# V rows kept at 32 columns a head in DRAM, padded by the stage that writes them

## The reference

```
k = (key @ Wk.T + bk);  v = (value @ Wv.T + bv)           # cross attention, key = value = context
scores = einsum('bqhd,bkhd->bhqk', q, k) * 16 ** -0.5
attn = softmax(scores);  out = einsum('bhqk,bkhd->bqhd', attn, v)
x = x + out @ Wo.T + bo
h = x' + causal_attention(rmsnorm(x', g1))                # x' = layernorm(x), rotary q and k, same head sizes
y = h + moe(rmsnorm(h, g2))                               # 8 experts, top 2
```

## Time and profile before

| | us |
|---|---|
| median of 3 runs | 3302.17 (3297.82 to 3305.19) |
| the profiled execution | 3297.82, its span 3296.2 |
| `project_inputs`, first and last instruction of its work | 22.5 to 284.7 |
| cross attention | 289.1 to 1656.7 |
| `project_self` | 1670.0 to 1898.6 |
| self attention | 1903.5 to 2292.8 |

### The profile page before, as it was taken

One profiled execution on the slowest core, in us unless ns is written; L12 is line 12 of the kernel. 1 busy time (PEld: TensorE's weight loads), 2 busy tenths in 40 slices (PEclk: granted clock), 3 DMA queues, 4 the chain that ended last, 5 costly groups with the idle time before them and its releaser, 6 DMA issues. The chain is left out here.

```text
span 3296.2 us, 55561 instructions
## 1 busy us (share of the span) xinstructions
PE 2698.5 (82%) x14654; PEld 1323.0 (40%) x14655; DVE 1763.2 (53%) x2832; ACT 1458.2 (44%) x2927; POOL 490.7 (15%) x650
## 2 busy tenths in 40 slices
PE   7996999999999999999949879887340299999980
PEld 5662232323232323233225434443340177777760
DVE  4565876767676767677436656664222022222223
ACT  2331576767676767677723336565010022222210
POOL 2444000000000000000014421110223300000006
PEclk9996899999999999999979979999665699999995
DMA  6777544444454444454035456653444211100116
GB/s 211 215 233 133 70 62 67 62 66 63 62 64 62 63 63 63 62 63 61 17 115 185 159 121 133 133 133 102 149 150 155 84 32 32 32 32 32 32 47 183
DMA packets 524784, 313.32 MB, mean 95 GB/s; under 512 B 312112, under 2 KB 486848, under 8 KB 524480
## 3 DMA queue, kind: packets, MB, share of 16 engines
q1 hardware_dynamic: 492752, 256.93, 38.6%
q0 software_dynamic: 11392, 37.76, 3.5%
q10 hardware_dynamic: 20464, 16.40, 1.6%
HBM read 188.91 MB, written 121.26 MB: 94 GB/s over the span
## 5 line engine op out<-in xcount | busy, mean ns | idle before, releaser
L719 DVE TENSOR_REDUCE att_cross_neg_max<-att_cross_ps_s 128x1 f32<-128x802 f32 x1024 | 965.6, 988 | 350.9 <-PE att_cross_ps_s L636 349.2
L794 ACT ACTIVATE att_cross_probs<-att_cross_ps_st 128x512 f32<-128x512 f32 (+1 forms) x1664 | 901.2, 599 | 394.7 <-PE att_cross_ps_st L655 382.2
L655 PE MATMUL att_cross_ps_st<-att_cross_q_pack,att_cross_k_pack 99*128 99x512 bf16 (+1 forms) x1664 | 575.0, 391 | 37.3 <-issue 28.4
L636 PE MATMUL att_cross_ps_s<-att_cross_k_pack,att_cross_q_pack 96*128 96x401 bf16 x2048 | 547.9, 350 | 70.1 <-DVE att_cross_neg_max L719 29.5
L670 PE MATMUL att_cross_ps_o<-att_cross_probs,att_cross_v_tiles 128*32 128x512 f32 (+1 forms) x3328 | 453.5, 618 | 1.0
L636 PEld LDWEIGHTS att_cross_ps_s<-att_cross_k_pack,att_cross_q_pack 96*128 96x128 bf16 x2048 | 176.8, 100 | 420.5 <-DVE att_cross_neg_max L719 204.9
L655 PEld LDWEIGHTS att_cross_ps_st<-att_cross_q_pack,att_cross_k_pack 99*128 99x128 bf16 (+1 forms) x1664 | 163.1, 100 | 415.5 <-ACT att_cross_probs L794 293.2
L719 DVE TENSOR_REDUCE att_self_neg_max<-att_self_ps_s 128x1 f32<-128x128 f32 (+3 forms) x512 | 236.2, 489 | 148.7 <-PE att_self_ps_s L639 145.7
L794 ACT ACTIVATE att_self_probs<-att_self_ps_st 128x256 f32<-128x256 f32 (+3 forms) x512 | 208.2, 441 | 142.4 <-PE att_self_ps_st L658 136.6
L1744 DVE COPY moe_hiddenT<-moe_ps_h 128x256 f32<-128x256 f32 x142 | 60.3, 425 | 296.9 <-PE moe_ps_h L1654 296.9
L636 PE MATMUL att_self_ps_s<-att_self_k_pack,att_self_q_pack 96*128 96x128 bf16 (+3 forms) x512 | 158.7, 312 | 56.4 <-DMA att_self_q_pack<-q_parts 25.1
(11 more groups left out here) (208 smaller groups left out, 2901.7 us busy)
## 6 DMA issues: line engine op xcount, KB each, us to landing
att_cross_k_pack<-k_parts SPq DMA_DIRECT2D x192, 200.1 KB, 7.5
k_parts<-in_part SPq DMA_DIRECT2D x72, 256.0 KB, 3.1
in_rows<-in_ctx_dram SPq DMA_DIRECT2D x24, 512.0 KB, 4.4
v_rows<-in_v_biased SPq DMA_DIRECT2D x24, 512.0 KB, 2.9
att_cross_q_pack<-q_parts SPq DMA_DIRECT2D x192, 64.0 KB, 7.7
att_cross_v_tiles<-v_rows SPq DMA_DIRECT2D x128, 96.0 KB
att_self_k_pack<-k_parts SPq DMA_DIRECT2D x192, 64.0 KB, 3.1
att_self_q_pack<-q_parts SPq DMA_DIRECT2D x192, 64.0 KB, 3.1
```

Of the source, the lines that this page charges most:

```text
L636: last = nc.tensor.matmul(ps_s[bank][:, n, 0:w], qp[v.buf][0:SROWS, j, q * P:(q + 1) * P], kp[v.buf][0:SROWS, j, s:s + w], start=True, sto ...
L655: mm = nc.tensor.matmul(ps_st[bank_of_step[s]][0:rows, q0:SEQ], kp[u.buf][0:MROWS, j, t * P:t * P + rows], qp[u.buf][0:MROWS, j, q0:SEQ], ...
L719: nc.vector.tensor_reduce(nmax[v.odd][:, col, half:half + 1], ps_s[bank][:, 0:len(spans), 0:spans[0][1]], AX.XY, ALU.max, negate=True).the ...
L794: nc.scalar.activation(pr[0:rows, (u.odd * STEPS + s) % RING, q0:SEQ], ps_st[bank_of_step[s]][0:rows, q0:SEQ], ACT.Exp).then_inc(exp_done, 1)
```

## The change

V is kept in DRAM as the attention reads it: 16 heads of 32 columns, ones and zeros included, so a row of `v_rows` grows from 1 KB to 2 KB. The stages that write V keep buffers of this shape, `v_pad`, set the ones and zeros in them once on DVE, and write each head's 16 numbers with a stride. The attention loads four heads (512 bytes a row) with one DMA for the full tiles and one for the rest, and no longer sets ones and zeros.

```diff
+        vpad = [p.sb(f"v_pad{i}", [P, QT, HEADS, VW]) for i in range(2)]       # project_inputs
-                            sp.dma_start(dst, vb[st.item % 2][0:st.size, 0, :])
+                            sp.dma_start(dst, vpad[st.item % 2][0:st.size, 0, :, :].rearrange("p h v -> p (h v)"))
...
             def _(dve):
+                for i in range(2):
+                    nc.vector.memset(vpad[i][:, :, :, HD:VW], 0.0).then_inc(pads, 1)
+                dve.wait_ge(pads, 2)
+                for i in range(2):
+                    nc.vector.memset(vpad[i][:, :, :, HD:HD + 1], 1.0).then_inc(pads, 1)
+                dve.wait_ge(pads, 4)
                 dve.sem_inc(xT_ready, 2)
...
-                        last = nc.vector.tensor_tensor(vb[st.item % 2][0:m, t, :], ps_v[0:m, t, :], ...
+                        last = nc.vector.tensor_tensor(vpad[st.item % 2][0:m, t, :, 0:HD],
+                                                       ps_v[0:m, t, :].rearrange("p (h d) -> p h d", d=HD), ...
...
-        VLOADS = 16 * GH * ((1 if kv >= P else 0) + (1 if kv % P else 0))      # attention
+        VLOADS = 16 * ((1 if kv >= P else 0) + (1 if kv % P else 0))
                 def load_v(v):
-                    for j in range(GH):
-                        src = v_rows[v.batch, :, v.columns.start + j * HD:v.columns.start + (j + 1) * HD]
-                        if kv >= P:
-                            sp.dma_start(va[v.vbuf][:, 0:kv // P, j, 0:HD], ...
+                    if kv >= P:
+                        sp.dma_start(va[v.vbuf][:, 0:kv // P, :],
+                                     v_rows[v.batch, 0:kv // P * P, v.columns].rearrange("(t p) v -> p t v", p=P))
+                    if kv % P:
+                        sp.dma_start(va[v.vbuf][0:kv % P, kv // P, :], v_rows[v.batch, kv // P * P:kv, v.columns])
...
-                for k in range(VBUFS):
-                    nc.gpsimd.memset(va[k][:, :, :, HD + 1:VW], 0.0).then_inc(ones_set, 1)
-                    nc.gpsimd.memset(va[k][:, :, :, HD:HD + 1], 1.0).then_inc(ones_set, 1)
...
                 def take_v(b):                                                  # project_self
-                    nc.scalar.copy(vs[:, :, :].rearrange("p (c t) d -> p c (t d)", c=KC), ps_t[:, :, :])
+                    for t in range(QT):
+                        last = nc.scalar.copy(vpad[:, t, :, 0:HD],
+                                              ps_t[:, t // 2, t % 2 * DIM:(t % 2 + 1) * DIM]
+                                              .rearrange("p (h d) -> p h d", d=HD))
...
-    v_rows = dram("v_rows", [batches, CTX, DIM])
+    v_rows = dram("v_rows", [batches, CTX, HEADS * VW])
-    v2_rows = dram("v2_rows", [batches, SEQ, DIM])
+    v2_rows = dram("v2_rows", [batches, SEQ, HEADS * VW])
```

More of the change, by code:

```diff
@@ L381, in take_v @@
                     for t, m in st.tiles():
-                        last = nc.vector.tensor_tensor(vb[st.item % 2][0:m, t, :], ps_v[0:m, t, :], keep["bv"][0:m, :],
-                                                       ALU.add)
+                        last = nc.vector.tensor_tensor(vpad[st.item % 2][0:m, t, :, 0:HD],
+                                                       ps_v[0:m, t, :].rearrange("p (h d) -> p h d", d=HD),
+                                                       keep["bv"][0:m, :].rearrange("p (h d) -> p h d", d=HD), ALU.add)
                     last.then_inc(v_ready, 1)
@@ L474, in attention @@
         qp = [p.sb(f"q_pack{i}", [P, GH, SEQ], BF16) for i in range(BUFS)]
-        va = [p.sb(f"v_tiles{i}", [P, NT, GH, VW]) for i in range(VBUFS)]
+        va = [p.sb(f"v_tiles{i}", [P, NT, GH * VW]) for i in range(VBUFS)]
         pr = p.sb("probs", [P, RING, SEQ])
@@ L521, in __init__ @@
                 self.rows = slice(g * GR, (g + 1) * GR)
-                self.columns = slice(g * GR, (g + 1) * GR)
+                self.columns = slice(g * GH * VW, (g + 1) * GH * VW)
                 self.odd = r % 2
@@ L670, in products @@
                         nc.tensor.matmul(ps_o[j * VW:(j + 1) * VW, q0:SEQ],
-                                         va[u.vbuf][0:rows, t, j, :],
+                                         va[u.vbuf][0:rows, t, j * VW:(j + 1) * VW],
                                          pr[0:rows, (u.odd * STEPS + t * GH + j) % RING, q0:SEQ],
@@ L933, in project_self @@
         v_sent = p.sem("v_sent")
+        pads = p.sem("pads")
         SENT = 16 * 3
@@ L1026, in _ @@
             def _(dve):
+                nc.vector.memset(vpad[:, :, :, HD:VW], 0.0)
+                dve.drain()
+                nc.vector.memset(vpad[:, :, :, HD:HD + 1], 1.0).then_inc(pads, 1)
                 for s in (on_ready, x1_ready, rope_read, *rest_ready):
@@ L1106, in take_v @@
                     act.wait_ge(v_sent, (b + 1) * 16)
-                    nc.scalar.copy(vs[:, :, :].rearrange("p (c t) d -> p c (t d)", c=KC), ps_t[:, :, :])\
-                      .then_inc(v_ready, 1)
+                    for t in range(QT):
+                        last = nc.scalar.copy(vpad[:, t, :, 0:HD],
+                                              ps_t[:, t // 2, t % 2 * DIM:(t % 2 + 1) * DIM]
+                                              .rearrange("p (h d) -> p h d", d=HD))
+                    last.then_inc(v_ready, 1)
                 def high(w, b):
```

28 lines of the change are left out of this document (14 added, 14 removed).

## The result

The changed kernel takes 3324.26 us (median of five, 3319.75 to 3327.92), against 3297.82 for the kernel before in the same session: a ratio of 1.0070, interval 1.0055 to 1.0086. It is slower by 26 us in the medians, by 23 by the ratio; I had forecast +5.5 us, 3307.7, in a range from 3298 to 3317.

What follows compares the result with a forecast made beforehand. The prediction took PE to set the pace in all four stages; 0 (cross) - 2 (self) + 5.5 (ring) + 2 (clock) = +5.5 us, giving 3303.3, or 3307.7 in the median's terms, range 3298 to 3317.

Steps and rivals of the forecast that it cites:

- V's loads in the self attention: Self attention: 4 DMAs a unit become 1, shortening PE's waits for the maxima rows; -2 us, bounds 0 and -6.5.
- V's loads in the cross attention: Cross attention: 8 DMAs a unit become 2, old and new price hidden under PE's work; 0 us.
- The ring: `project_self`: V's larger store delays the h0 store's landing and next residual, 1.37 us in four turns; +5.5, bounds 0 and +11.3.
- PE's clock in `project_self`: `project_self`: PE's pause before L994 grows to 2.8 us, so the granted clock falls once; +2 us.
- New memsets: Projections and `project_self`: new DVE memsets of 2.4 and 1.2 us stay hidden; 0 us.
- DVE's stride: Projections, bias add L382: strided writing of V costs 0, upper bound 12 us; as a rival 3318 us, chance 0.05.
- POOL's memsets: Memsets that leave POOL: PE comes to its first product long after them; 0 us.
- V's store in the projections: Projections: store 13.1 MB larger, DMA share from 0.74 to about 0.87 of 1.08; 0 us.
- ACT's four strided copies: `project_self`: ACT's copy of 1.01 us becomes four, at most 1.6 us, before a 4.33 us gap; 0 us.
- The slower one: Rival in `project_self`: larger store at 185 GB/s or two clock falls, +9 to +12.5, 3311 to 3315 us; chance 0.23.
- The faster one: Rival: self attention's maxima rows come in time in every unit (-6.5), V's store hidden; 3295.7 us, chance 0.10.
- The condition under which I had called the prediction wrong: Wrong if ring keeps 23.6 us, L382 grows, or PE's waits in either attention change by more than 6.5 us.

Runs made afterwards that it cites:

- v_store_last: Changed kernel with V's store in `project_self` issued behind those of x1 and h0: 3319.20 us against 3302.00 for the kernel before, ratio 1.0051.
- pads_on_pool: Changed kernel with the two padding memsets of `project_self` on POOL instead of DVE: 3311.59 us against 3292.86 for the kernel before, ratio 1.0060.
- half_load: Changed kernel with V's self-attention load cut to its first two tiles, the others set to ones: 3305.44 us against 3292.86 for the kernel before, ratio 1.0044.
- best_plain: Kernel before, unpadded; four k/q loads ahead of the maxima rows, eight behind, V's load last; V's store last, cross start gated: 3281.64 us, ratio 0.9963.
- split_loads: Changed kernel with V loaded by head, same doubled bytes in 128-byte rows: 3304.48 us against 3299.60 for the kernel before, ratio 1.0015.
- best_padded: Changed kernel; four k/q loads ahead of the maxima rows, V's load last; V's store last, memsets on POOL, cross start gated: 3282.63 us, ratio 0.9970.
- all_three: Changed kernel with V's store last, self-attention k/q loads behind the maxima rows, both attention starts gated: 3294.40 us against 3302.00, ratio 0.9975.
- before_all_three: Kernel before, V unpadded, with V's store last, self-attention k/q loads behind the maxima rows, both attention starts gated: 3291.39 us against 3302.00, ratio 0.9969.
- self_only: Change in `project_self` and self attention only, projections and cross attention as before: 3321.13 us against 3299.60 for the kernel before, ratio 1.0064.

## Why the prediction was wrong, point by point

- **V's loads in the self attention, -2: the step that failed.** Wrong in sign, and at 14.6 us the largest loss. I had read that SP comes to the k loads sooner and that the rows travel among the k and q loads, and still priced V's shorter engine time as a gain. What counts is how much SP has issued ahead of ACT's small DMA, and both parts of the change raised it, V's bytes and the earlier k and q loads: 384 to 704 KB. The 14.6 us are 8.7 of PE's waits, 1.3 between the first product and the first with V (a pause of 1.0 us and 1.6 us more at the low clock are in it), and three stretches of 3.4 us at a granted clock of 0.50, an estimated 5.1 us of PE's pace; together 15.1. My bounds, 0 and -6.5, left out a loss because I bounded a wait by its own size: a wait can be taken away only once, but it can grow in the 20 units that had none.
- **V's loads in the cross attention, 0.** Right for the 31 units in step (0.6 us lost between first and last). The two prices were both low: the window of 61 GB/s did not hold the whole load, and 382 GB/s was not reached. By the packets of one unit's V, 410 KB in pieces of 64 bytes keep the 16 engines busy for 4.4 us, not 3.9, and 820 KB in pieces of 512 bytes for 2.9, not 2.1. Wrong at the start, which I never asked about: 5.5 us, PE behind the rows for which it had been in time.
- **The ring, +5.5.** Right in mechanism and nearly in size: 6.2 us from first to last residual; the four turns named grew by 1.5 to 1.7 us each, where 1.37 was forecast, at 385 GB/s. v_store_last undoes it.
- **PE's clock in `project_self`, +2.** It stayed at 1.00 through the turns; the lateness was split between two pauses, of 1.86 and 1.47 us in the turn shown, where I had put it all on one. That was in part chance: pads_on_pool, with the same code in the ring, had a pause of 2.20 us and 3.4 us at 0.50 behind it. The clock fell in the self attention instead, after waits of only 1.09 to 1.24 us, shorter than the 1.46 us at which I had called it safe, and such a fall lasted 3.4 us, not the 13 I had priced.
- **New memsets, 0.** Hidden in the projections (PE's first wait 6.14 against 6.11 us). Not in `project_self`: SP's first load waits for DVE's signal, which stands behind the memsets. That is 1.1 us, in every kernel with them on DVE; I had looked at the loads' landing, not at what lets SP issue them. PE's first products then took 6.51 us, not 5.46, as more of them ran before the clock rose, but half_load and best_plain show that this goes either way with and without the memsets.
- **DVE's stride, POOL's memsets, V's store in the projections, 0 each.** Right: 414 ns, and a share of 0.87. ACT's four strided copies took 1.20 us together, under the 1.6 allowed.
- **Rivals.** The slower one I named, a ring at 185 GB/s or two falls of the clock, did not happen (one turn of 25.3 us passed its mark of 25.2, at 385 GB/s); its sign did, for another cause. The faster one named the right wait with the wrong sign. The condition under which I had called the prediction wrong, PE's waits in either attention changing by more than 6.5 us, is the one that was met, by 8.7 us in the self attention.

The Trainium skill's 512-byte rule (DMA: Bandwidth & Descriptors, Specifications), under which these loads should gain, holds for the rate: the window of 6 us with V's burst (396 to 402, the first k and q packets in it too) carries 170 GB/s at the same share of 0.65 as 61 before. For the time it is beside the point: split_loads went back to short rows and gained some 20 us.

Open stays why the self stage varies so much with the same code (391.0, 393.6, 395.1 and 401.6 us, waits of 13.0 to 22.2), and what the rows' last 4 us are. POOL's expert weights are a candidate for these, but no run here moved or left them out. Nor was it tried to send the rows from SP's queue.

## What to carry to other kernels

When a change makes a queue's DMAs fewer or larger, ask what SP issues sooner because of it, and which small transfer of another engine, sent late and needed soon, then stands behind it: count the KB issued ahead of that one. Put bulk loads that have slack behind the small one that has none; here the order on the queues, V's store included, was worth more (10 to 11 us) than any layout of V (1 us between best_padded and best_plain, 3 us between all_three and before_all_three). A wait seen in some turns of a loop is the edge of a slack, so bound it upwards by the turns that don't wait yet; and look at the first unit of each stage by itself.

## What the runs showed of the hardware

```profile
q1 hardware_dynamic: 606, 0.94, 94.3%
q0 software_dynamic: 71, 0.27, 14.0%
...
q10 hardware_dynamic: 51, 0.01, 5.1%
```

The data is what is late: no packet of the rows moves until 349.53, 8.9 us after the issue, when the ninth of the ten loads ahead of them lands (349.57). Before, the first moves at 342.04, 2.2 us after the issue. From the last packet to the complete semaphore it is 0.9 us here and some 2.1 before, so the signal adds nothing to the difference. In the self attention about 0.4 us of lateness is likewise there at the first packet (2.05 to 2.46 us). The Trainium skill (DMA: Bandwidth & Descriptors, Queues, rings and completion order) says both that each engine goes round the queues, and that the write which raises a DMA's semaphore lands only after every earlier write of that engine, across its queues. The first is not what this start shows, if the rows' packets were ready to be moved soon after the issue; the second would make the signal late, not the data. What holds the packets back is not shown.

The granted clock fell from 1.00 to 0.50 after a pause of 1.24 us at 2041.76, and came back within 3.4 us; in the kernel before, a pause of 1.23 us at 2101.88 left it at 1.00. The last pause of `project_self`, 1.36 us, was followed by 3.4 us at 0.50 in self_only, before_all_three and best_padded, and by none in the kernel before. So the length of the pause alone does not tell.
